# A decoder layer in one kernel: the eight scatters of a token tile go in three groups behind TensorE's signals, and VectorE normalises the probabilities ahead of the first query bias

## The chip, the cores and the metric

The kernel runs on one core of a Trainium2 chip. The metric is the device time of one execution in microseconds (us). Before the change three timed runs gave 1859.75 to 1864.37 us, median 1863.71.

## What is computed

The reference is a decoder layer on 4096 tokens (64 sequences of 64) of 256 numbers, with a layer norm after each of three parts:

```python
x = layernorm(x + self_attention(x))          # causal, one head, its own norm ahead of it and its own residual
x = layernorm(x + cross_attention(x, ctx))    # 16 query heads, 4 key/value heads, RMS norm of q and k
x = layernorm(x + ffn(x))                     # 64 experts, the 8 best of each token, and a shared expert

# cross attention
q = rmsnorm(x @ Wq + bq); k = rmsnorm(ctx @ Wk + bk); v = ctx @ Wv + bv
out = softmax(q @ k.T * scale + mask) @ v @ Wo
# ffn
logits = x @ gate_w.T; topv, topi = top_k(logits, 8); w = softmax(topv)
out = sum_e w_e * (silu(x @ g_e.T) * (x @ u_e.T)) @ d_e.T + sigmoid(x @ s) * shared(x)
```

## The kernel before

The work is in three phases: attention with routing, experts, and the sum of the experts' results. The change is in the first.

**Tiles and steps.** The 4096 tokens are 32 tiles of 128. A step of the attention phase works on six tiles at once, each in another stage: a is the newest tile, then b, c, d, e, f, each one tile older. `pipeline` writes out the first six and the last steps and runs those between as a loop with two steps in its body; half way (behind `MIDDLE`) the loop is cut, and VectorE has three more operations in `place` for each tile from there on. For each engine a function `step` lists by hand what it does in a step, in order; engines wait for each other on semaphores alone. Each engine works its list strictly in order, so whatever stands behind a wait waits too.

**TensorE in a step.** The part around the change: it transposes the self attention's result of c (`x1_transpose`) and the normalised input rows of a (`x_transpose`, L594, signal `xn_transposed`), multiplies the joined heads of e with Wo (`cross_output`, L754, 48 matmuls, signal `cross_proj`), and projects the queries of c in four groups of four heads (`query_project`, L602, signal `q_projected`). The fourth group reuses the PSUM bank of the first, and so waits until VectorE has added the first bias (`q_biased`). Then come the transposes of the self attention's probabilities of b and the cross attention's of d (`cross_probs_transpose`, L729, behind `cross_probs`), the key and value projections of c, the first product with the values of d, and, in the next step, the transposes of the normalised queries (`query_transpose`, L699) in two halves: the first behind VectorE's `query_norm` (L1037), the second behind POOL's `scale_queries` (L537).

**VectorE in a step.** Behind the choice of the experts' slots (`place`, whose last operation L1185 sorts the eight slots of a token into the row buffer, signal `slots_sorted`), it masks the cross scores of d and subtracts the maximum, sums the exponentials (`cross_sum`), adds the residual of e to the product with Wo and takes its moments (`x2_add`, L1080 and following), adds the first two query biases (L1027), normalises the probabilities of d (`cross_normalise`, L1067), takes the low part of the context (`ctx_low`, L944), adds the other two biases, and goes on with sums of squares, the key's bias and the norm of the first half of the queries.

**ScalarE** squares the queries group by group behind each bias and takes the high part of the context (`ctx_high`), on which `ctx_low` waits.

**POOL (GpSimd) in a step.** It computes the reciprocal roots as powers (L507: for keys, input, residuals, and the queries in two halves), scales keys and the second half of the queries, and scatters tile f: each token's row of 272 numbers goes to the eight slots of its experts in DRAM, by eight indirect DMAs of 128 rows each (`scatter`, L562), whose descriptors POOL writes. Ahead of the first stand four waits for the parts of the row. `wait_alone` is a wait that also counts up a semaphore that nobody reads, so that it stays an instruction of its own. Six scatters stand ahead of `power_h2` (the root for e's residual norm) and two behind it; then come the powers of the queries of c.

**SyncE** loads inputs and stores rows, and in the first half of the loop also clears pages of the slot table in DRAM.

## Time and profile before

| | us |
|---|---|
| median of three timed runs | 1863.71 |
| their range | 1859.75 to 1864.37 |
| profiled execution: span from first to last instruction | 1858.0 |
| attention phase, up to about | 1120 |
| expert phase, up to about | 1746 |
| sum of the experts' results, to the end | 1858 |

The page gives no own time of the profiled execution beside its span; the span stands 5.7 us under the median of the timed runs. In the profile, an engine's row carries its start, its length, the engine, the line, the operation with what it writes and reads, and in brackets how long the engine had been idle before it and what ended that. TensorE's ends are modelled: its row tells when its work should be done, not when its signal reached another engine. A row of POOL's scatter tells how long POOL wrote descriptors, not how long the rows travelled.

### The profile page before, as it was taken

How to read it: one execution, taken by the hardware profiler on the slowest of the kernel's cores; microseconds unless marked ns; L12 is line 12 of the kernel's file. 1: busy time of each engine (PE TensorE's matmuls, PEld its weight loads, DVE VectorE, ACT ScalarE, POOL GpSimd, SP SyncE). 2: the span in 40 equal slices, each digit the busy share in tenths (PEclk: the TensorE clock that was granted, in tenths of full speed). 3: DMA queues.
4: the chain of work that ended last, by engine and by line, in shares of the span. 5: the costliest groups of instructions: out<-in, count | busy, mean ns of one | idle time of the engine just before them, and what ended most of it. 6: DMA issues, size and time to landing. Idle time of an engine off the chain costs nothing. (4 is left out here: it accounts for less than half of the span.)

```text
span 1858.0 us, 34769 instructions
## 1 busy us (share of the span) xinstructions
PE 1532.2 (82%) x9744; PEld 1252.6 (67%) x9744; DVE 1259.3 (68%) x3827; ACT 688.5 (37%) x1526; POOL 1050.2 (57%) x1023
## 2 busy tenths in 40 slices
PE   4899989899998898989999864787877777777696
PEld 3688878777787787878788753565655555555464
DVE  3788888787888888888888744345555555433397
ACT  3444444343444434344343412232322322322254
POOL 3457666676766666666676633555555455555321
PEclk8799999999999999999999866889898998988799
DMA  7422232222222121211212484655555555554596
GB/s 248 136 81 100 80 102 68 91 86 89 90 85 96 46 74 51 67 60 46 82 45 73 101 280 139 192 162 154 163 178 165 177 165 162 175 170 137 189 418 281
DMA packets 182739, 246.40 MB, mean 133 GB/s; under 512 B 30732, under 2 KB 159321, under 8 KB 178148
## 3 DMA queue, kind: packets, MB, share of 16 engines
q1 hardware_dynamic: 148948, 169.71, 29.4%
q0 software_dynamic: 27648, 69.28, 10.2%
q10 hardware_dynamic: 6032, 6.13, 1.0%
q8 instruction: 46, 0.75, 0.2%
q14 instruction: 65, 0.53, 0.1%
HBM read 136.19 MB, written 117.19 MB: 136 GB/s over the span
## 5 line engine op out<-in xcount | busy, mean ns | idle before, releaser
L1571 POOL DMA_INDIRECT expert_out_scratch<-y,target x320 | 316.6, 989 | 297.7 <-DVE y L1797 199.9
L562 POOL DMA_INDIRECT slot_scratch<-xrow x256 | 260.5, 1018 | 188.9 <-DVE xrow L1185 117.4
L1630 PE MATMUL bank_g<-gu,x_turned 128*128 (+1 forms) x1408 | 218.8, 305 | 15.9 <-issue 13.7
L1630 PEld LDWEIGHTS bank_g<-gu,x_turned 128*128 128x128 f32 x1408 | 196.8, 216 | 30.8 <-issue 30.4
L1689 ACT ACTIVATE x_turned<-bank_x 128x512 f32<-128x512 f32 x176 | 105.3, 599 | 281.1 <-PE bank_x L1612 161.3
L1649 PE MATMUL bank_y<-dp,inter_t 64*128 (+1 forms) x352 | 136.8, 473 | 84.7 <-DVE y L1797 59.5
L507 POOL TENSOR_TENSOR q_rs<-q_ve,minus_half 128x8 f32<-128x8 f32 x64 | 137.4, 2147 | 114.9 <-DVE q_ve L1016 111.4
L754 PE MATMUL bank_d<-wo_w,o2t 128*128 128x256 f32 x1536 | 196.0, 288 | 2.0 <-DVE o2t L944 2.0
L754 PEld LDWEIGHTS bank_d<-wo_w,o2t 128*128 128x128 f32 x1536 | 190.3, 196 | 2.7 <-DVE o2t L944 2.7
L1788 DVE TENSOR_TENSOR inter<-silu,bank_g 128x128 f32<-128x128 f32 x176 | 50.2, 285 | 207.6 <-ACT silu L1696 144.9
L1797 DVE COPY y<-bank_y 128x512 f32<-128x512 f32 x160 | 110.2, 689 | 103.9 <-remote 72.0
L602 PE MATMUL bank_c<-wq_w,x1t 128*128 128x512 f32 x576 | 147.8, 401 | 24.5 <-DVE q_work L1027 21.2
L828 ACT ACTIVATE q_work<-q_work 128x512 f32<-128x512 f32 x128 | 80.0, 631 | 219.3 <-DVE q_work L1027 182.5
L1612 PE MATMUL bank_x<-identity,x_rows 128*128 128x128 f32 x704 | 127.7, 309 | 24.6 <-DMA x_rows<-token_row_scratch 24.6
L1612 PEld LDWEIGHTS bank_x<-identity,x_rows 128*128 128x128 f32 x704 | 82.7, 153 | 90.6 <-issue 90.6
L602 PEld LDWEIGHTS bank_c<-wq_w,x1t 128*128 128x128 f32 x576 | 105.9, 191 | 54.7 <-DVE q_work L1027 30.0
L1649 PEld LDWEIGHTS bank_y<-dp,inter_t 64*128 64x128 f32 x352 | 57.3, 203 | 121.9 <-issue 121.3
L1651 PE MATMUL bank_y<-dp,inter_t 64*128 64x256 f32 x352 | 137.5, 474 | 0.0
L719 PEld LDWEIGHTS bank_c<-k2t,stage_b 128*128 128x128 f32 x1024 | 123.2, 200 | 11.3 <-issue 11.3
L719 PE MATMUL bank_c<-k2t,stage_b 128*128 128x64 f32 x1024 | 127.7, 286 | 0.4 <-ACT stage_b L817 0.4
L699 PE MATMUL bank_c<-identity,q_work 128*128 128x128 f32 x512 | 70.5, 282 | 47.8 <-DVE q_work L1037 45.1
L1696 ACT ACTIVATE silu<-bank_g 128x128 f32<-128x128 f32 x176 | 49.1, 279 | 153.1 <-PE bank_g L1630 106.7
(245 smaller groups left out, 3412.6 us busy)
## 6 DMA issues: line engine op xcount, KB each, us to landing
x_rows<-slot_scratch SPq DMA_DIRECT2D x320, 136.0 KB
results<-expert_out_scratch SPq DMA_DIRECT2D x32, 1024.0 KB, 8.8
slot_scratch<-zeros SPq DMA_DIRECT2D x16, 816.0 KB, 4.2
dp<-in_down SPq DMA_DIRECT2D x161, 64.0 KB
slot_scratch<-zeros SPq DMA_DIRECT2D x8, 1088.0 KB, 9.1
gu<-in_gate_up SPq DMA_DIRECT2D x11, 768.0 KB
expert_out_scratch<-y,target POOLq DMA_INDIRECT x320
token_row_scratch<-xrow SPq DMA_DIRECT2D x32, 136.0 KB
```

The costliest lines, as they stand in the source:

```text
L507: nc.gpsimd.tensor_tensor(out_, base, minus_half[:, 0:width], ALU.pow).then_inc(sig[done], 1)
L562: nc.gpsimd.indirect_dma_start(out=slot_d[:, :], out_offset=bass.IndirectOffsetOnAxis(ap=xrow[slot][:, SLOT8 + k:SLOT8 + k + 1].bitcast(U3 ...
L602: last = nc.tensor.matmul(target, left[a][:, c, :], right(b, c), start=(n == 0 and c == 0), stop=(n == len(PASSES) - 1 and c == C - 1))
L719: last = nc.tensor.matmul(bank_c[:, n, p * S:(p + 1) * S], q2t[:, n, 2 * p:2 * p + 2, :].rearrange("p h s -> p (h s)"), k2t[:, p // 2, n * ...
L754: last = nc.tensor.matmul(bank_d[:, 0, 0:D], o2t[a][:, h, :], wo_w[b][:, h, :], start=(n == 0 and h == 0), stop=(n == len(PASSES) - 1 and ...
L1571: nc.gpsimd.indirect_dma_start(out=y_d[:, :], out_offset=bass.IndirectOffsetOnAxis(ap=target[n % 8][:, j:j + 1], axis=0), in_=y[s % 4][:, ...
L1612: mm = nc.tensor.transpose(bank_x[:, s % 2, (2 * j + c) * P:(2 * j + c + 1) * P], x_in[s % 8][:, j, c * P:(c + 1) * P], identity[:, :])
L1630: mm = nc.tensor.matmul(bank_g[:, s % 2, j * P:(j + 1) * P], xt[s % 2][:, j, c, :], w, start=(c == 0), stop=(c == C - 1))
L1649: nc.tensor.matmul(bank_y[:, 0, 0:D], inter_t[s % 2][0:INNER, :], dp[0:INNER, bass.ds(own, D)], start=True, stop=True)
L1651: nc.tensor.matmul(bank_y[:, 1, 0:D], inter_t[s % 2][INNER:P, :], dp[INNER:P, ring * D:(ring + 1) * D], start=True, stop=True).then_inc(si ...
L1689: nc.scalar.activation(xt[s % 2][:, :, :, :].rearrange("p j c n -> p (j c n)"), bank_x[:, s % 2, :], ACT.Copy).then_inc(sig["x_copied"], 1)
L1797: nc.vector.tensor_copy(y[s % 4][:, :, :], bank_y[:, :, 0:D])\
```

## The change

It has three parts. On POOL the eight scatters are split into four, two and two. The four now also wait until TensorE has transposed the input rows of tile a, the next two until it has finished the output projection of e, and the last two, which stood directly behind `power_h2`, until it has finished the fourth query projection of c. On VectorE the normalisation of the probabilities and the context's low part go ahead of the first two query biases. On ScalarE the context's high part goes ahead of the first square.

```diff
@@ POOL, step
                 at(d, bias_values)
-                for k in range(6):
+                at(a, turned_rows)
+                for k in range(4):
+                    at_slot(f, scatter, k)
+                at(e, joined_heads)
+                for k in range(4, 6):
                     at_slot(f, scatter, k)
                 at(e, power_h2)
+                at(c, joined_queries)
                 for k in range(6, TOP_K):
                     at_slot(f, scatter, k)
                 at(c, power_queries, 0)
...
+            def turned_rows(t):
+                wait_alone(pool, sig["xn_transposed"], t + 1, sig["pool_held"])
+
+            def joined_heads(t):
+                wait_alone(pool, sig["cross_proj"], t + 1, sig["pool_held"])
+
+            def joined_queries(t):
+                wait_alone(pool, sig["q_projected"], 4 * t + 4, sig["pool_held"])
@@ ScalarE, step
-                at(c, square_queries, 0)
                 at(c, ctx_high)
+                at(c, square_queries, 0)
                 at(c, square_queries, 1)
@@ VectorE, step
                 at(e, x2_add)
+                at(d, cross_normalise)
+                at(c, ctx_low)
                 at(c, query_bias, 0)
                 at(c, query_bias, 1)
-                at(d, cross_normalise)
-                at(c, ctx_low)
                 at(c, query_bias, 2)
```

POOL in the loop, from the value bias of d to the first power of the queries of c. `slot_scratch` is the slot table in DRAM, `xrow` the row buffer, `h_rs` and `q_rs` the roots. Before:

```order
L551 TENSOR_TENSOR v<-v_new,bkv_b 128x512 [waits cross_out,v2_copied]
L101 REGISTER_ALU
L562 DMA slot_scratch<-xrow 208897x272 [waits x2_normed,token_named,shared_gate,slots_sorted]
L562 DMA slot_scratch<-xrow 208897x272 x5
L507 TENSOR_TENSOR h_rs<-h_ve,minus_half 128x1 [waits h2_var]
L562 DMA slot_scratch<-xrow 208897x272 x2
L506 ISA
L507 TENSOR_TENSOR q_rs<-q_ve,minus_half 128x8 [waits q_var]
```

And in the changed kernel:

```order
L551 TENSOR_TENSOR v<-v_new,bkv_b 128x512 [waits cross_out,v2_copied]
L562 DMA slot_scratch<-xrow 208897x272 [waits xn_transposed,x2_normed,token_named,shared_gate,slots_sorted]
L562 DMA slot_scratch<-xrow 208897x272 x3
L562 DMA slot_scratch<-xrow 208897x272 [waits cross_proj]
L562 DMA slot_scratch<-xrow 208897x272
L507 TENSOR_TENSOR h_rs<-h_ve,minus_half 128x1 [waits h2_var]
L101 ISA
L562 DMA slot_scratch<-xrow 208897x272 [waits q_projected]
L562 DMA slot_scratch<-xrow 208897x272
```

Two scatters more stand behind a signal of the output projection, and the last two behind one of the query projections; the powers stand where they stood.

VectorE in the loop, from the sum of the exponentials of d to the first sum of squares of c. `stage_b` holds the probabilities, `q_work` the queries, `ctxt` the context. Before:

```order
L1063 RECIPROCAL s_rec<-s_sum 128x16 [waits cross_sum]
L1080 TENSOR_TENSOR h<-x_res,bank_d 128x256 [waits x1_res_loaded,cross_proj]
L947 BN_STATS h_stat<-h 128x6 [waits h2_done]
L949 BN_AGGR h_mv<-h_stat 128x2 [waits h2_stats]
L951 TENSOR_SCALAR h_ve<-h_mv 128x1 [waits h2_moments]
L1027 TENSOR_TENSOR q_work<-bank_c,bq_b 128x512 [waits q_projected] x2
L1067 TENSOR_TENSOR stage_b<-stage_b,s_rec 128x1024 [waits cross_recip]
L944 TENSOR_TENSOR ctxt<-ctx_in,ctxt 128x256 [waits ctx_hi]
L1027 TENSOR_TENSOR q_work<-bank_e,bq_b 128x512 [waits q_projected]
```

And in the changed kernel, whose lines there are numbered 14 higher:

```order
L965 TENSOR_SCALAR h_ve<-h_mv 128x1 [waits h2_moments]
L1081 TENSOR_TENSOR stage_b<-stage_b,s_rec 128x1024 [waits cross_recip]
L958 TENSOR_TENSOR ctxt<-ctx_in,ctxt 128x256 [waits ctx_hi]
L1041 TENSOR_TENSOR q_work<-bank_c,bq_b 128x512 [waits q_projected] x2
L1041 TENSOR_TENSOR q_work<-bank_e,bq_b 128x512 [waits q_projected]
```

The normalisation and the context's low part now stand between the moments of the residual and the first query bias, and nothing stands between the second bias and the third.

## Rows read from the trace of the kernel before

**Rows 1.** Busy time of each engine in the window 161 to 1007 us.

```profile
core 0: us, PE busy (x) PEld busy (x) DVE busy (x) ACT busy (x) POOL busy (x), PEclk, DMA share, GB/s
161.00:1007.00 846.00, 768.50 (x5230) 669.56 (x5229) 697.05 (x1662) 358.10 (x702) 564.28 (x517) 0.99 0.22 75
```

**Rows 2.** Timeline of TensorE: starts of the cross output projection in four steps.

```profile
161.55 0.71 PE L754 MATMUL bank_d<-wo_w,o2t 128*128 128x256 f32 x4
944.26 0.95 PE L754 MATMUL bank_d<-wo_w,o2t 128*128 128x256 f32 x6
975.07 1.20 PE L754 MATMUL bank_d<-wo_w,o2t 128*128 128x256 f32 x8
1038.50 1.19 PE L754 MATMUL bank_d<-wo_w,o2t 128*128 128x256 f32 x8
```

**Rows 3.** Waits, 161 to 1007 us: total, times, longest.

```profile
PE bank_c L699 <- DVE q_work L1037: 36.3, 24, 2.0
DVE h L1080 <- remote: 31.6, 14, 3.3
PE bank_c L602 <- DVE q_work L1027: 21.2, 20, 1.6
PE bank_d L729 <- DVE stage_b L1067: 17.4, 10, 2.3
```

**Rows 4.** Timeline of TensorE, 500 to 600 us: start, length, idle before.

```profile
517.13 0.38 PE L594 MATMUL bank_a<-identity,x_n 128*128 128x128 f32 x2
517.27 6.00 PE L754 MATMUL bank_d<-wo_w,o2t 128*128 128x256 f32 x48
528.77 1.68 PE L602 MATMUL bank_c<-wq_w,x1t 128*128 128x512 f32 x6 [1.40 <-DVE q_work L1027]
549.58 5.99 PE L754 MATMUL bank_d<-wo_w,o2t 128*128 128x256 f32 x48
564.78 1.09 PE L729 MATMUL bank_d<-identity,stage_b 128*128 128x128 f32 x8 [2.26 <-DVE stage_b L1067]
```

**Rows 5.** Timeline of VectorE, 500 to 570 us.

```profile
516.86 0.23 DVE L1185 MAX8 xrow<-meta 128x8 uint32<-128x64 f32 x1
526.67 0.42 DVE L1080 TENSOR_TENSOR h<-x_res,bank_d 128x256 f32<-128x256 f32 x1 [3.24 <-remote]
528.03 1.29 DVE L1027 TENSOR_TENSOR q_work<-bank_c,bq_b 128x512 f32<-128x512 f32 x2
529.23 1.22 DVE L1067 TENSOR_TENSOR stage_b<-stage_b,s_rec 128x1024 f32<-128x1024 f32 x1
530.70 0.68 DVE L1027 TENSOR_TENSOR q_work<-bank_e,bq_b 128x512 f32<-128x512 f32 x1
536.18 1.21 DVE L1037 TENSOR_TENSOR q_work<-q_work,q_rs 128x1024 f32<-128x1024 f32 x1
557.22 0.42 DVE L1080 TENSOR_TENSOR h<-x_res,bank_d 128x256 f32<-128x256 f32 x1 [0.36 <-remote]
```

**Rows 6.** Timeline of POOL, 500 to 600 us, and one scatter at 955.

```profile
517.98 1.06 POOL L562 DMA_INDIRECT slot_scratch<-xrow  x1 [2.44 <-DVE xrow L1185]
521.94 0.97 POOL L562 DMA_INDIRECT slot_scratch<-xrow  x1 [0.31 <-issue]
524.49 0.98 POOL L562 DMA_INDIRECT slot_scratch<-xrow  x1 [0.30 <-issue]
528.92 1.04 POOL L562 DMA_INDIRECT slot_scratch<-xrow  x1 [0.20 <-issue]
533.40 1.81 POOL L507 TENSOR_TENSOR q_rs<-q_ve,minus_half 128x8 f32<-128x8 f32 x1 [2.11 <-DVE q_ve L1016]
536.35 2.55 POOL L507 TENSOR_TENSOR q_rs<-q_ve,minus_half 128x8 f32<-128x8 f32 x1
555.36 0.98 POOL L562 DMA_INDIRECT slot_scratch<-xrow  x1 [0.30 <-issue]
955.14 1.72 POOL L562 DMA_INDIRECT slot_scratch<-xrow  x1 [0.19 <-issue]
```

More of the change, by code:

```diff
@@ L912, in step @@
                 at(d, cross_exp)
+                at(c, ctx_high)
                 at(c, square_queries, 0)
-                at(c, ctx_high)
                 at(c, square_queries, 1)
```

## The prediction

> **What bounds the kernel now.** I read the windows first, then the waits of the attention loop, and the timelines of TensorE, VectorE and GpSimd (POOL) over two neighbouring steps. In the window 161 to 1007 us, which holds 26 steady steps of the attention loop, TensorE is busy 768.5 of 846.0 us, 91%, and every other engine less [rows 1]. The change touches nothing outside that loop, so I need the step: from 161.55 to 1038.50 us TensorE starts the cross output projection 28 times, which makes 27 steps of 32.48 us [rows 2].
>
> The waits say where TensorE stands still in those steps: 36.3 us before the transposes of the queries (L699, for VectorE's normalised queries), 21.2 us before the fourth query projection (L602, for a query bias), 17.4 us before the transposes of the probabilities (L729, for their normalisation) [rows 3]. 74.9 us in all is the most that this change can reach. The fourth row shows why: 14 times VectorE sat before its residual add, 31.6 us in all, for a "remote" event.
>
> The timeline of one step names that event. TensorE's output projection starts at 517.27 and takes 6.00 us, so it ends at 523.27 (I call this moment T0) [rows 4]. VectorE's add, which waits for it, starts at 526.67, 3.4 us later, after 3.24 us idle [rows 5]. In the next step the projection ends at 555.57 and the add starts at 557.22, 1.65 us later. So the lateness is none of TensorE's own work; it comes and goes. What moves against T0 is POOL's train of scatters: it starts at 517.98, the fourth at 521.94, the sixth at 524.49 [rows 6], and the add starts 2.2 us behind the sixth; in the next step T0 falls into the fourth scatter, of 555.36, and the add starts 1.9 us behind that one. I read it so: **a long train of scatters holds back TensorE's completion signals until the train has drained.** The bias behind the add is late, and with it the fourth projection, which starts at 528.77 = T0 + 5.5 [rows 4].
>
> **The change, part by part.**
>
> *Normalisation ahead of the first query bias (VectorE).* In the second step the normalisation stands behind two late biases, and TensorE waits 2.26 us for it [rows 4]. Behind the add it is done some 3 us after the add, before the fourth projection ends. The 17.4 us go. In return the first bias starts later by what normalisation and the context's low part take, 529.23 to 530.70 = 1.47 us [rows 5], and the fourth projection waits for that bias. ScalarE's swap only makes the context's high part early enough for this; ScalarE idles there, so it costs nothing.
>
> *Four scatters behind the turned rows (POOL).* The transposes of x end at 517.13 + 0.38 = 517.51 [rows 4]. From the last signal to the first scatter POOL needs 0.89 us (slots sorted at 516.86 + 0.23, scatter at 517.98) [rows 5, 6]. The new wait stands ahead of four satisfied ones, so the first scatter starts at 518.4 to 518.6 instead of 517.98, the fourth 3.96 us behind it, at 522.4 to 522.6. T0 still falls into the fourth. The train now ends there. Its signal then comes 1.9 to 2.2 us after the fourth start (the two values above): 1.0 to 1.5 us after T0. Where VectorE sorts the slots later than that (in the second half of the loop it has three more operations ahead of them), the wait costs nothing and the whole train is later. I take the add at T0 + 1.5.
>
> *Two scatters behind the output projection.* They start 0.9 us after its signal, when the first train has drained; such a pair on its own held nothing in the traced step (scatters from 528.92 on, and VectorE's rows show no idle time from 528.03 to 536.18). The power for the residual's norm waits behind them, until about T0 + 4.8; its reader on VectorE stands behind the fourth bias, which can't start before T0 + 6.8, so it costs nothing. If the second bias's signal were caught by them, rival 3 has the price.
>
> *Two scatters behind the last query projection.* That projection ends at 528.77 + 1.68 = 530.45 (call it G) [rows 4]. The pair starts at G + 0.9 and takes one period and one length, (524.49 - 521.94) / 2 + 1.04 = 2.3 us [rows 6]; the first power of the queries can start at G + 3.2. Now it starts at 533.40 = G + 2.95. The chain behind it on POOL (two powers, the key's square and scale, the second half's scale) sets TensorE's second transposes, so +0.25 us a step is the upper bound. Against it stands this: the biases 3 and 4 no longer wait behind the normalisation, so VectorE starts its norm of the queries (536.18, G + 5.7) as soon as the first power ends, about G + 5.0 [rows 5]. POOL's second power took 2.55 us where it started 0.17 us behind that norm, the first 1.81 us [rows 6]. In the new order it starts at G + 6.1, when the norm is nearly over; if overlap is what lengthens it, it gains 0.7 us and the step 0.45. Between +0.25 and -0.45 I take 0, as nothing in this trace shows the second power without the norm.
>
> The Trainium skill (SBUF — State Buffer, "SBUF: two separate sides") says that a VectorE operation with two inputs in SBUF and a GpSimd operation that reads SBUF exclude each other for the whole instruction. The 2.55 us agree with it; by the rule alone the step would be 0.45 us shorter still, 27 times that is 12 us, and the forecast 1835.5.
>
> **The sum.** New step: add at T0 + 1.5; add to bias, 526.67 to 528.03 = 1.36 [rows 5]; normalisation and context 1.47; bias to fourth projection, 528.03 to 528.77 = 0.74; together 5.1. That projection 1.68. From its end to the next T0 (530.45 to 555.57) 25.1. In all 31.88 us against 32.48, 0.60 us less; over 27 steps 16.2 us. The span goes from 1858.0 to 1841.8. The median of the timed runs, 1863.7, lies 5.7 above the span; taken along, **1847.5 us** (0.9% less). The own range of this case, with the add between T0 + 1.2 and T0 + 1.9 and the chain within -0.45 and +0.25, is 1827 to 1865, most of it below 1858. A measurement of this kernel tells about 0.3%, 5.6 us, from no change.
>
> **Rivals.**
>
> *1. The signals come at once.* Four scatters may be too few to hold TensorE. For it: a step exists in which TensorE never waits for a bias nor for probabilities, from 944.26 to 975.07, 30.81 us [rows 2]. Against it: in the second step the signal was caught in the fourth scatter already. All steps at 30.8 give 27 x 1.67 = 45 us less: about 1818.
>
> *2. Slower: the lateness does not come from the scatters.* Then the add stays where it is, on the average of the two steps T0 + 2.5, and the 1.47 us put ahead of the first bias hit the fourth projection in full: 2.5 + 1.36 + 1.47 + 0.74 = 6.1, a step of 6.1 + 1.68 + 25.1 = 32.9, 0.4 more than now, 27 times that is 11 us: 1874.5. It decides from an add at about T0 + 2.1 on. Against it: the lateness ends 2 us after a scatter's start in both steps.
> The Trainium skill (same page and section) says that the engines' ports and the DMAs' are separate and that a DMA cannot be slowed by a compute operation, nor the reverse. By that rule scatters would not touch TensorE's signals and this rival would hold; the 3.24 us of [rows 5] speak against reading it so widely.
>
> *3. Nothing gained: POOL becomes the limit.* The last pair starts 0.9 us behind G, and if it catches the key projection's signal, which falls into it, or stretches under VectorE's work, as the first scatter of such a pair did at 955.14 (1.72 us for 1.04) [rows 6], the power moves to G + 3.6 or later. With +0.6 on the chain the gain is gone: 32.48, that is about 1864. For it: POOL's chain from the first power to the second half's scale has no slack, since TensorE's 36.3 us of [rows 3] hang on it.
>
> **Numbers.** My forecast 0.50, rival 1 0.17, rival 2 0.13, rival 3 0.20. The forecast's case is nearly all faster by more than 5.6 us, rival 1 wholly, rival 3 mostly same, rival 2 slower: faster 0.64, same 0.20, slower 0.16. The range takes in rival 1 down to 1814 and rival 2 up to its centre, 1874.
>
> **What would show it.** In the profile of the changed kernel: the wait L729 for the normalisation gone; VectorE's idle time before the residual add 1 to 1.5 us a step instead of 0.4 to 3.3; TensorE's wait before the fourth query projection 0.9 to 1.1 us in nearly every step (near nothing: rival 1; 1.5 and more: rival 2); the first query power at G + 3.2 and the second shorter than 2.55 us or not; the step 31.9 us. TensorE waiting for POOL's scale of the queries before the second transposes would be rival 3. I am wrong if the signals of the second and third projection are held by the middle pair, or if the step shrinks by more than 1 us.

## The result, and the profile after

| | before | changed |
|---|---|---|
| median of the timed runs, us | 1861.82 (20 runs) | 1867.22 (20 runs) |
| their range | 1848.98 to 1872.33 | 1858.24 to 1873.57 |
| span of the profiled execution | 1858.0 | 1871.6 |

The changed kernel is slower by 0.4%: ratio 1.0038, 95% interval 1.002 to 1.0057. Forecast were 1847.5 us and 0.9% less. Of the 13.6 us between the two spans, 5.6 lie in the 27 steps of the loop, 2.1 before them and 5.8 behind the last one, where the change touches nothing; those last two vary from run to run, as the medians differ by 5.4 us alone, no more than the loop. So the question is why the 16.2 us did not come.

In the changed kernel line numbers in the loop are 14 higher: L768 is the output projection, L616 the query projection, L713 the transposes of the queries, L743 those of the probabilities.

Timeline of TensorE of the changed kernel, first and last start of the output projection, against [rows 2]:

```profile
163.69 0.48 PE L768 MATMUL bank_d<-wo_w,o2t 128*128 128x256 f32 x2
1046.26 0.96 PE L768 MATMUL bank_d<-wo_w,o2t 128*128 128x256 f32 x6
```

882.57 / 27 = 32.69 us a step, against 32.48 before and 31.88 forecast. The 27 steps as a window, before and then changed (columns as in [rows 1]):

```profile
161.55:1038.50 876.95, 794.82 (x5406) 692.02 (x5405) 723.80 (x1722) 370.35 (x725) 584.66 (x534) 0.99 0.22 74
```

```profile
163.70:1046.20 882.50, 805.86 (x5405) 707.09 (x5403) 743.96 (x1724) 371.93 (x725) 593.32 (x534) 0.97 0.22 74
```

The granted clock is the news: 0.97 where it was 0.99. For the same 5406 matmuls TensorE is busy 805.9 us instead of 794.8, 11.1 more. The waits, 161 to 1007 us (total, times, longest), against [rows 3]:

```profile
PE bank_c L713 <- DVE q_work L1051: 50.0, 26, 2.1
PE bank_c L616 <- DVE q_work L1041: 19.4, 18, 1.6
DVE h L1094 <- PE bank_d L768: 7.5, 12, 0.8
DVE h L1094 <- remote: 3.0, 8, 0.4
```

The wait for the probabilities (17.4 us) is gone, VectorE's wait before the add fell from 31.6 to 10.5 us, and the wait for a bias stayed near 20. The wait before the transposes of the queries grew by 13.7 us. Waits alone make the kernel faster by 17.4 + 1.8 - 13.7 = 5.5 us. The 11.1 us of longer busy time outweigh that, and the difference, 5.6 us, is what the loop grew by.

Timeline of TensorE over two neighbouring steps (start, length, idle before):

```profile
519.31 5.99 PE L768 MATMUL bank_d<-wo_w,o2t 128*128 128x256 f32 x48
529.48 1.66 PE L616 MATMUL bank_c<-wq_w,x1t 128*128 128x512 f32 x6
538.56 1.07 PE L713 MATMUL bank_c<-identity,q_work 128*128 128x128 f32 x8 [1.99 <-DVE q_work L1051]
539.60 2.34 PE L616 MATMUL bank_a<-qkv_w,xnt 128*128 128x512 f32 x12
550.48 6.00 PE L768 MATMUL bank_d<-wo_w,o2t 128*128 128x256 f32 x48
561.64 1.68 PE L616 MATMUL bank_c<-wq_w,x1t 128*128 128x512 f32 x6 [1.06 <-DVE q_work L1041]
570.66 1.77 PE L713 MATMUL bank_c<-identity,q_work 128*128 128x128 f32 x8 [1.89 <-DVE q_work L1051]
572.51 3.17 PE L616 MATMUL bank_a<-qkv_w,xnt 128*128 128x512 f32 x12
584.21 5.99 PE L768 MATMUL bank_d<-wo_w,o2t 128*128 128x256 f32 x48
```

The first step is 31.17 us long, the second 33.73. In the second the fourth projection waits 1.06 us for its bias, as forecast, and 1.89 us of idle time follow before the transposes; then these take 1.77 us for 1.07, and the projection behind them 3.17 for 2.34. The windows of the two places say why (the 0.55 is the clock):

```profile
539.60:544.00 4.40, 4.40 (x32) 3.99 (x31) 2.73 (x12) 3.14 (x8) 4.32 (x5) 1.00 0.00 0
570.50:574.00 3.50, 3.34 (x14) 3.08 (x15) 2.57 (x7) 1.05 (x2) 3.42 (x4) 0.55 0.00 0
```

TensorE ran at 1.2 GHz there. 13 of the 27 steps have such a stretch, against 4 before. As (1 - granted clock) x length, summed over it, the loop lost 23.9 us to it, before 6.8. That is an upper measure: what runs slowly ahead of a wait only shortens the wait. In the kernel before two steps with the same wait for the probabilities (2.1 us) took 27.18 us from G, the end of the fourth query projection, to the next T0 with such a stretch behind it, and 27.14 without: the wait for the queries, 1.4 us in the second, was gone in the first; in the changed kernel the stretches stand behind the last long wait, and a step takes 26.87 instead of 25.3.

Timeline of POOL, the same two steps, against [rows 6] (four, two, two):

```profile
520.83 1.06 POOL L562 DMA_INDIRECT slot_scratch<-xrow  x1 [3.49 <-issue]
525.01 0.98 POOL L562 DMA_INDIRECT slot_scratch<-xrow  x1 [0.30 <-issue]
526.69 0.97 POOL L562 DMA_INDIRECT slot_scratch<-xrow  x1 [0.70 <-issue]
532.14 1.04 POOL L562 DMA_INDIRECT slot_scratch<-xrow  x1 [2.21 <-PE bank_c L616]
534.47 1.69 POOL L507 TENSOR_TENSOR q_rs<-q_ve,minus_half 128x8 f32<-128x8 f32 x1
...
556.24 0.97 POOL L562 DMA_INDIRECT slot_scratch<-xrow  x1 [0.30 <-issue]
566.53 1.71 POOL L507 TENSOR_TENSOR q_rs<-q_ve,minus_half 128x8 f32<-128x8 f32 x1
568.20 1.05 POOL L533 TENSOR_TENSOR k2s<-k 128x512 f32<-128x512 f32 x1
569.37 2.55 POOL L507 TENSOR_TENSOR q_rs<-q_ve,minus_half 128x8 f32<-128x8 f32 x1
```

And VectorE:

```profile
525.94 0.42 DVE L1094 TENSOR_TENSOR h<-x_res,bank_d 128x256 f32<-128x256 f32 x1 [0.72 <-PE bank_d L768]
536.19 2.07 DVE L1051 TENSOR_TENSOR q_work<-q_work,q_rs 128x1024 f32<-128x1024 f32 x1 [0.62 <-POOL q_rs L507]
558.12 0.42 DVE L1094 TENSOR_TENSOR h<-x_res,bank_d 128x256 f32<-128x256 f32 x1 [0.39 <-remote]
567.72 1.57 DVE L1030 TENSOR_SCALAR q_ve<-q_ss 128x8 f32<-128x8 f32 x1
569.20 1.21 DVE L1051 TENSOR_TENSOR q_work<-q_work,q_rs 128x1024 f32<-128x1024 f32 x1
```

The add stands at T0 + 0.6 and T0 + 1.6 (T0 = 525.30, 556.48). In the second step (G = 563.32) the first power starts at G + 3.2 and ends at 568.24, but the norm of the queries starts 0.96 us later, at G + 5.9: VectorE still stands in L1030, 1.57 us long where the same operation for the first half takes 0.17, until POOL's square of the keys (568.20 + 1.05) is done. In the first step (G = 531.14) the norm starts as the power ends, at G + 5.05, and takes 2.07 us for 1.21. Either way it ends at G + 7.1. Each of the 27 steps is of one kind or the other: 20 have the long L1030 (1.6 to 1.8 us), 7 the long norm.

### The profile page after: what moved, and what is told of

Its sections match the earlier page's. It is cut to its first block and busy times, and to the rows that moved or that the text cites. A ratio compares the mean times of both kernels' runs of the same rounds, so it can differ in the third digit from the quotient of the medians.

```text
span 1871.6 us, 34891 instructions
## 1 busy us (share of the span) xinstructions
PE 1547.4 (83%) x9744; PEld 1269.1 (68%) x9744; DVE 1279.8 (68%) x3827; ACT 690.5 (37%) x1526; POOL 1060.4 (57%) x1023
## 5 line engine op out<-in xcount | busy, mean ns | idle before, releaser
L562 POOL DMA_INDIRECT slot_scratch<-xrow x256 | 270.1, 1055 | 280.4 <-issue 101.5
L768 PE MATMUL bank_d<-wo_w,o2t 128*128 128x256 f32 x1536 | 196.5, 289 | 2.0 <-DVE o2t L958 2.0
L768 PEld LDWEIGHTS bank_d<-wo_w,o2t 128*128 128x128 f32 x1536 | 190.7, 196 | 2.7 <-DVE o2t L958 2.7
L616 PE MATMUL bank_c<-wq_w,x1t 128*128 128x512 f32 x576 | 150.9, 408 | 24.1 <-DVE q_work L1041 20.3
L616 PEld LDWEIGHTS bank_c<-wq_w,x1t 128*128 128x128 f32 x576 | 107.2, 194 | 56.2 <-DVE q_work L1041 29.0
L713 PE MATMUL bank_c<-identity,q_work 128*128 128x128 f32 x512 | 75.5, 296 | 62.5 <-DVE q_work L1051 60.1
L713 PEld LDWEIGHTS bank_c<-identity,q_work 128*128 128x128 f32 x512 | 61.9, 151 | 69.0 <-issue 54.3
```

What stands on the lines that cost most here:

```text
L562: nc.gpsimd.indirect_dma_start(out=slot_d[:, :], out_offset=bass.IndirectOffsetOnAxis(ap=xrow[slot][:, SLOT8 + k:SLOT8 + k + 1].bitcast(U3 ...
L616: last = nc.tensor.matmul(target, left[a][:, c, :], right(b, c), start=(n == 0 and c == 0), stop=(n == len(PASSES) - 1 and c == C - 1))
L713: last = nc.tensor.transpose(bank_c[:, h // 4, (h % 4) * P:(h % 4 + 1) * P], q2s[:, n * half + h, :], identity[:, :])
L768: last = nc.tensor.matmul(bank_d[:, 0, 0:D], o2t[a][:, h, :], wo_w[b][:, h, :], start=(n == 0 and h == 0), stop=(n == len(PASSES) - 1 and ...
```

## The experiments

T0 and G are as in the prediction. "Half clock" is the time lost to it in all 27 steps, by the upper measure above. The kernels ran on three chips; each is compared with the kernel before on its own chip. On which chip the first profiles were taken is not on record; by its time, 1862 us, it is like chip 1. The changed kernel was not run on chip 1, and the kernel before was timed there but has no trace.

| kernel | chip | ratio to before (95%) | step | fourth projection at T0 + | first power at G + | G to next T0 | half clock |
|---|---|---|---|---|---|---|---|
| before (first profile) | | | 32.48 | 4.90 | 3.7 | 25.95 | 6.8 |
| changed (first profile) | | 1.0038 | 32.69 | 4.87 | 3.3 | 26.16 | 23.9 |
| e1, groups only | 1 | 0.978 (0.975 to 0.981) | 31.48 | 4.25 | 3.3 | 25.66 | 6.8 |
| e2, normalisation only | 1 | 1.010 (1.006 to 1.014) | 33.47 | 6.44 | 2.3 | 24.79 | 34.1 |
| e3, changed, wait filled | 1 | 0.989 (0.985 to 0.993) | 32.09 | 4.97 | 3.3 | 25.49 | 3.4 |
| e4, before, wait filled | 1 | 1.001 (0.998 to 1.004) | 32.71 | 5.22 | 3.4 | 25.81 | 8.5 |
| e5, changed, keys squared on ScalarE | 2 | 1.007 (1.004 to 1.009) | 30.64 | 4.46 | 3.3 | 24.55 | 3.4 |
| e6, before, the same | 2 | 0.988 (0.985 to 0.991) | 29.71 | 3.97 | 2.4 | 24.21 | 1.7 |
| e7, changed again | 3 | 1.033 (1.031 to 1.036) | 32.30 | 4.52 | 3.3 | 26.15 | 23.9 |
| e8, groups only, the same square | 3 | 0.998 (0.996 to 1.000) | 30.09 | 3.95 | 3.3 | 24.60 | 1.7 |
| e9, one wait | 3 | 1.001 (0.998 to 1.003) | 30.17 | 3.97 | 2.4 | 24.66 | 1.7 |
| e10, two waits | 3 | 1.016 (1.013 to 1.019) | 31.02 | 3.97 | 3.3 | 25.52 | 5.1 |
| e11, before again | 3 | one run | 30.17 | 3.97 | 2.4 | 24.67 | 1.7 |
| e12, e6 again | 3 | 0.988 (0.986 to 0.990) | 29.73 | 3.97 | 2.4 | 24.22 | 1.7 |
| e13, e8 again | 3 | 0.996 (0.994 to 0.998) | 30.09 | 3.95 | 3.3 | 24.60 | 1.7 |
| e14, one wait, the same square | 3 | 0.989 (0.987 to 0.990) | 29.73 | 3.97 | 2.4 | 24.22 | 1.7 |
| e15, normalisation only, again | 3 | 1.008 (1.005 to 1.011) | 30.66 | 4.66 | 2.2 | 24.37 | 0 |
| e16, e14 again | 3 | 0.994 (0.992 to 0.996) | 29.73 | 3.97 | 2.4 | 24.22 | 1.7 |

Columns four to seven are means over the 27 steps of one profile. The kernel before took a median of 1880.11 us on chip 1, 1619.21 on chip 2 and 1617.62 to 1622.72 on chip 3.

**e1, the groups alone.** The change without its edits on VectorE and ScalarE:

```diff
-                at(d, cross_normalise)
-                at(c, ctx_low)
                 at(c, query_bias, 0)
                 at(c, query_bias, 1)
+                at(d, cross_normalise)
+                at(c, ctx_low)
```

> POOL's groups as in the change, VectorE's and ScalarE's order as before. Theory A (the lost time is TensorE's clock: in the changed kernel the wait before the query transposes is 1.9 us instead of 1.6, and in 13 of 27 steps the granted clock then falls to 1.2 GHz for one stretch of 3.4 us, 1.6 us a step): the wait before the transposes stays at or above 1.9 us where the query power starts at G + 3.2, the dips come as in the changed kernel or fewer where other waits share the step; the probabilities' wait L729 comes back with 10 to 17 us; span 1860 to 1880. Theory B (the groups alone are worth their time, the order of VectorE costs it): faster than before by 5 to 15 us.

1835.45 us, 45 less than the kernel before on this chip: more than theory B's 5 to 15, and nothing of theory A's 1860 to 1880. TensorE's waits from the first to the last start of the output projection:

```profile
PE bank_c L713 <- DVE q_work L1051: 47.8, 27, 2.5
PE bank_c L616 <- DVE q_work L1041: 6.6, 5, 1.8
PE bank_d L743 <- DVE stage_b L1081: 1.7, 2, 0.9
```

The waits for a bias and for probabilities are nearly gone without the new order on VectorE. Grouping alone is worth 2.2% on this chip, and the wait before the transposes is nearly as long as in the changed kernel (1.8 us a step against 1.9), so it is not the new order that makes it; e9 and e10 show the last pair of scatters in its place.

**e2, the normalisation alone.** The kernel before with only the edits on VectorE and ScalarE.

> VectorE's and ScalarE's order as in the change, POOL's six and two as before. Both theories: the output projection's signal is late by up to 3.3 us again, so the fourth query projection starts at T0 + 6.1 in such steps and waits 2 us. Theory A: 0.4 us a step more than before, about 11 us slower than before, and dips follow the longer waits. Theory B: slower than the changed kernel by as much as the groups are worth.

1896.49 us. TensorE's waits, same stretch:

```profile
PE bank_c L602 <- DVE q_work L1027: 62.4, 26, 3.4
PE bank_c L699 <- DVE q_work L1037: 18.9, 27, 1.9
```

With signals late, each bias is 1.5 us later still: the wait for it triples against [rows 3]. The wait behind it shrinks, but more than the 17.4 us for the probabilities is given back, and 20 of 27 steps have a half-clock stretch, most of them over the late fourth projection, which takes up to 2.9 us there for 1.7.

**e3 and e4, the wait filled.** 13 transposes of the identity matrix, into a bank that the queries' transposes overwrite, stand in the wait before these; e3 on the changed kernel, e4 on the one before. The extra transposes are work the reference does not ask for.

```diff
+                    for k in range(FILL):
+                        nc.tensor.transpose(bank_c[:, 0, 0:P], identity[:, :], identity[:, :])
+                pe.wait_ge(sig["q_normed_b" if n else "q_normed_a"], t + 1)
```

> The changed kernel with 13 transposes of the identity, whose result nobody reads, in TensorE's wait before the query transposes (about 1.4 of the 1.9 us). Every other wait and order is as in the change. Theory A: the dips of the granted clock in the loop go from 13 steps to 3 or fewer, the steps with a dip (33.7 us) become 31.2 to 32.2 us, and the time falls by about 10 x 1.6 = 16 us or more below the changed kernel, so below before as well. Theory B (the clock falls for another reason and has no part in it): the time stays within 4 us of the changed kernel.

> The kernel before with the same 13 transposes in the same wait. Theory A: before has only 4 steps with a dip in the loop, so at most 4 x 1.6 = 6 us are to be had; where the wait is 1.5 us, 13 transposes of 0.11 us just fill it. Gain 2 to 7 us. If filling is worth the same here as in the changed kernel, the clock isn't what separates the two.

e3 took 1858.03 us, e4 1879.16. The waits and the windows of the loop, e3 and then e4:

```profile
PE bank_c L617 <- DVE q_work L1043: 23.5, 19, 1.8
PE bank_c L715 <- DVE q_work L1053: 8.9, 27, 0.5
```

```profile
167.31:1033.62 866.31, 827.73 (x5757) 727.25 (x5756) 751.85 (x1722) 370.82 (x725) 591.42 (x534) 1.00 0.22 75
```

```profile
166.46:1049.65 883.19, 836.55 (x5758) 729.54 (x5756) 723.76 (x1722) 369.24 (x725) 582.79 (x534) 0.99 0.22 74
```

Nothing that VectorE or POOL do in e3 is earlier (add at T0 + 1.34, first power at G + 3.3, norm over at G + 7.1, as in the changed kernel), TensorE only does more; yet the step falls from 32.69 to 32.09, since one step instead of 13 has a half-clock stretch. That is 0.60 x 27 = 16 us, about what theory A gave. The two steps compared come from different runs and perhaps chips, but the steps of the changed kernel's own trace agree (26.87 against 25.3 from G to the next T0, as above). The same filling gives the kernel before nothing that stands clear of the noise (1.001, of 2 to 7 us expected); the clock costs it little. So the clock is the greater part of what went missing. Even so e3 stays 1.2% behind e1 on the same chip: that is the price of the new order on VectorE.

**e5 and e6, the keys squared on ScalarE.** POOL's square of the keys goes to ScalarE, e5 on the changed kernel, e6 on the one before:

```diff
             def square_keys(t):
-                pool.wait_ge(sig["k_biased"], t + 1)
-                nc.gpsimd.tensor_tensor(k2s[:, :, :], k2[:, :, :], k2[:, :, :], ALU.mult).then_inc(sig["k_squared"], 1)
+                act.wait_ge(sig["k_biased"], t + 1)
+                nc.scalar.activation(k2s[:, :, :], k2[:, :, :], ACT.Square).then_inc(sig["k_squared"], 1)
```

> The changed kernel with the squares of the keys taken by ScalarE (behind its copy of the values) instead of by POOL between the two query powers. Theory A': the norm of the queries on VectorE (two inputs in SBUF) starts 0.96 us behind the first power because POOL's key square, which reads SBUF, stands there first and shuts it out; without it the norm starts at G + 5.0 instead of G + 5.9 and TensorE's wait before the query transposes falls from 1.9 to about 1.0 us; POOL's chain is shorter by up to 1.03 us too. The step falls by 0.8 to 1.0 us and the dips of the clock become rare: 30 to 45 us less than the changed kernel. Rival: the norm waits for something else (it stays at 0.96 behind the power); then only POOL's chain gets shorter and, as that has 0.2 us of slack, the step stays within 0.3 us.

> The same edit on the kernel before. Theory A': norm of the queries at G + 4.9 instead of G + 5.7 at best, as VectorE's own chain (biases 3 and 4 behind the normalisation, which the change had moved) takes until then: 0 to 0.8 us a step, 0 to 20 us less than before. If the change's order is worth what it was meant to be, the fifth kernel is faster than this one by 10 us or more.

These two fell on another chip, on which the kernel before needs 1619.21 us. VectorE and POOL in e5, one step:

```profile
510.64 0.69 DVE L1041 TENSOR_TENSOR q_work<-bank_c,bq_b 128x512 f32<-128x512 f32 x1 [0.67 <-PE bank_c L611]
515.62 1.23 DVE L1051 TENSOR_TENSOR q_work<-q_work,q_rs 128x1024 f32<-128x1024 f32 x1 [0.58 <-POOL q_rs L507]
```

```profile
513.88 3.32 POOL L507 TENSOR_TENSOR q_rs<-q_ve,minus_half 128x8 f32<-128x8 f32 x2
```

The norm starts at G + 5.0 in every step now and takes 1.23 us: what my forecast gave it with the square still on POOL. The wait before the transposes is 1.0 us instead of 1.9, and one step has a half-clock stretch instead of 13. e6 beats the kernel before by 1.2%; e5 stays behind it, and behind e6 by 1.9%, the reverse of the 10 us that the change was to be worth. How much e5 gains on the changed kernel itself can't be said, as that was not run on this chip.

The two powers of e5 also answer what the forecast left open. The second one starts 0.06 us ahead of the norm and takes 1.64 us, with the norm at 1.23 beside it. In e6, where it starts 0.17 us behind the norm in all steps but one, it takes 2.55. So not the overlap lengthens it: it depends on which of the two starts first.

**e7 to e10, the parts on a third chip.** e7 is the changed kernel. e8 is e1 with the square on ScalarE. e9 and e10 are e1 with fewer waits:

```diff
-                at(a, turned_rows)
```

in e10, and in e9 also

```diff
-                at(c, joined_queries)
```

> The changed kernel itself, as the measure for the three others on the same chip. 0.2 to 0.6% slower than before, with 10 or more steps of the loop that have a stretch at 1.2 GHz.

> The four, two, two of POOL with VectorE's and ScalarE's order as before (the first experiment's kernel), and the keys squared by ScalarE. Theory: the fourth query projection starts at T0 + 3.95 without a wait in the first half of the loop, and the norm of the queries directly behind the first power: TensorE's wait before the query transposes 1.0 us instead of 1.8, a step 29.9 us instead of 30.8, 20 to 28 us under the first experiment's kernel, if both are run on one chip. Rival: without POOL's key square the second power starts beside the norm and takes 2.55 us again, and the chain's slack is used up; then 10 us or less.

> As the first experiment, but only the wait for the output projection's signal is kept, between the fourth scatter and the fifth; the first four and the last two wait for no signal of TensorE. Theory C (a pause before the fifth scatter is what frees the signal): the add starts at T0 + 0.1 to 1.8 as in the first experiment, and the fourth projection at T0 + 3.95. The last two scatters follow the residual's power at once: query power back at G + 2.95, the step 0.1 to 0.3 us shorter, unless the four scatters in a row hold the signals of the third and fourth projection (biases 3 and 4 late by 1 to 2 us, 0.5 to 1.5 us a step more). So 0.972 to 0.980 of before, or up to 1.00 if they do.

> As the first experiment without the wait for the transposed input rows. Theory C: that wait moves the first scatter by 0 to 0.8 us (from 0.47 to 1.28 us behind the transposes in every second step) and no signal of TensorE falls between; without it the four are over earlier, so the add in those steps is as prompt as with it or more so: within 0.3% of the first experiment's 0.978. If the wait matters, the add is late by 1 us or more in every second step and the ratio is above 0.985.

1673.77, 1617.21, 1621.03 and 1644.26 us, the kernel before 1618.48. Here the change costs 3.3%, where 0.2 to 0.6% was expected. Of 0.972 to 0.980 for e9 and about 0.978 for e10 nothing came either: both counted on the gain of chip 1. The wait for the output projection ahead of the fifth scatter costs nothing and gains nothing (e9). The wait for the queries ahead of the last pair, with which e10 is at 1.016 and without which e9 is at 1.001, costs 1.4%: the first power moves from G + 2.4 to G + 3.3, and with it the next T0 by 0.86 us.

**e11, the kernel before on that chip.**

> The kernel before, for its trace on this chip. If this chip is one of those on which the kernel before needs about 1619 us, both theories expect that TensorE's signals come within 0.1 us of its modelled ends all through the train of six scatters, that the fourth query projection starts at T0 + 3.95 in nearly every step, and that the first query power starts at G + 2.2 to 2.4 (T0: end of the output projection, G: end of the fourth query projection). If it is one that needs 1860 to 1880 us: signals late by up to 3 us behind the fourth scatter, fourth projection at up to T0 + 5.5, as in the first trace. A third outcome, late signals together with a short time or the reverse, would part the two and say that the chip's slowness is not what makes the signals late.

1616.6 us, in one run. An output projection and VectorE around its end, and POOL's train in the same step:

```profile
490.63 6.00 PE L754 MATMUL bank_d<-wo_w,o2t 128*128 128x256 f32 x48
496.52 0.25 DVE L1063 RECIPROCAL s_rec<-s_sum 128x16 f32<-128x16 f32 x1
496.77 0.42 DVE L1080 TENSOR_TENSOR h<-x_res,bank_d 128x256 f32<-128x256 f32 x1
```

```profile
491.34 1.06 POOL L562 DMA_INDIRECT slot_scratch<-xrow  x1 [2.45 <-DVE xrow L1185]
496.57 0.97 POOL L562 DMA_INDIRECT slot_scratch<-xrow  x1 [0.30 <-issue]
497.85 0.97 POOL L562 DMA_INDIRECT slot_scratch<-xrow  x1 [0.31 <-issue]
```

T0 is 496.63, and the six scatters stand against it as they do in the first step of [rows 4, 6]: the fifth just ahead of it, the sixth 1.22 us behind. There the add came 3.40 us after T0, here it comes 0.14 us after it, with POOL at the fifth scatter and the sixth still to come. TensorE's waits from first to last start:

```profile
PE bank_c L699 <- DVE q_work L1037: 29.1, 27, 1.5
PE bank_e L711 <- DVE logits L1099: 3.7, 1, 3.7
```

No wait for a bias, none for probabilities: the 21.2 and 17.4 us of [rows 3], which the change was to work on, do not exist on this chip. The signals are late on one chip and punctual on another, with the same program; a train of scatters alone does not make them late. Nor are the scatters slower to travel on the one than on the other: from 161 to 977 us their 9600 packets took 9.3% of the 16 DMA engines' time before, and in e11 10368 took 10.0%, the same for each.

**e12 to e14, what could beat both.** The square on ScalarE in the kernel before (e12, as e6), with the groups (e13, as e8), and with one wait (e14, e9 with the square).

> The kernel before with the keys squared on ScalarE. Theory C, that VectorE's norm of the queries stands behind POOL's square of the keys on any chip: about 1 us a step less, 27 steps, on 1619 us a ratio of 0.985 to 0.990 as before. On a chip with late signals the power itself starts later, the norm behind it, and the same 1 us a step remains: 0.983 to 0.990. Rival D, that the gain is a smaller share of TensorE at half clock: nothing on a chip where the kernel before keeps its clock.

> Grouped scatters alone, with the keys squared on ScalarE. On a chip whose signals are not late, theory (grouping gains nothing there and the last pair's wait puts the first power at G + 3.2 instead of G + 2.2): within 0.4% of the kernel before, the two edits cancelling. On a chip whose signals are late: both gain, 0.960 to 0.970. Rival (the two edits take the same idle time): no better than the grouping alone, 0.978.

> Scatters behind one signal only (the fifth behind the output projection, the other seven as before), normalisation where it was before, keys squared on ScalarE. On a chip without late signals: that of the key square alone, 0.985 to 0.990, as one wait there cost nothing. On a chip with late signals: the first train is four, so the first biases come as with the full grouping, and the first power is not held to G + 3.2: 0.955 to 0.970, the best of all. Rival: the train of four that follows the wait catches the signal of the third projection, and the result is no better than the kernel before with the key square.

1601.75, 1616.39 and 1603.62 us, the kernel before 1622.72. Moving the square is worth 1.2% on two chips; in the kernel before it saves 0.45 us a step rather than the full 1 us, 12 of the 21 us between the medians, so that the ratio fell into the expected range in part by luck. The 0.45 are just what the norm of the queries gains in the mean of the steps (G + 5.11 to G + 4.66); there VectorE's own list sets when it starts. In e12 it directly follows L1016:

```profile
534.05 0.17 DVE L1016 TENSOR_SCALAR q_ve<-q_ss 128x8 f32<-128x8 f32 x1
534.13 1.22 DVE L1037 TENSOR_TENSOR q_work<-q_work,q_rs 128x1024 f32<-128x1024 f32 x1
```

The full grouping gives 0.8 of that back. None of the three was run on chip 1, so whether one wait with the square is the best where signals are late stays open.

**e15 and e16.** e2 and e14 again.

> Only the normalisation ahead of the first query bias, scatters six and two as before. On a chip without late signals: normalisation and context put 0.6 to 1.3 us ahead of the fourth query projection (T0 + 4.5 to 5.2 instead of 3.95), the first power stays at G + 2.2, so no half-clock stretches are added: 27 steps by 0.6 to 1.3 us are 16 to 35 us, a ratio of 1.010 to 1.022. That and the 1.6% which the last pair's wait cost there make up the 3.3% of the changed kernel. Rival: the clock falls here as well (10 steps or more with a half-clock stretch) and the ratio is 1.025 or more, which would make the order on VectorE alone the cause of the fall. On a chip with late signals: 1.010 as in the first run.

> One wait (fifth scatter behind the output projection), normalisation where it was, keys squared on ScalarE. On a chip without late signals 0.985 to 0.990, as before. On a chip with late signals 0.955 to 0.970: the first train is four scatters there, the biases come at T0 + 1.5 and 3.1 as with the full grouping, and the norm of the queries follows the first power at once. Rival: the six scatters behind the fourth run into one another there and hold the signals of the third and fourth query projection, 0.985 or more.

1627.76 and 1609.07 us, the kernel before 1617.62. The new order on VectorE costs 0.8% here, with no half-clock stretch at all, less than the 1.010 that I gave as the lower end: in about half of the steps of the loop's first half the bias has room. e16 is 0.6% faster than before, outside the 0.985 to 0.990 expected, and e14, the same program, 1.1%, with intervals that just miss each other. Their steps are alike to the hundredth (29.73); e16's median is 5 us higher and that of the kernel before 5 us lower than in e14's comparison. So half a per cent between two such comparisons tells nothing of the loop.

## Why the prediction was wrong

**On the chip of the first profile.** By its own sum, 5.1 + 1.68 + 25.1 = 31.88:

- *The fourth projection at T0 + 5.1.* Measured 4.87 in the mean of 27 steps, 4.1 to 4.2 and 5.2 by turns in the first half. With its length G stands at T0 + 6.53, against 6.78. Right, a little on the safe side: the add came at T0 + 1.34 instead of 1.5, where its mean before was 2.31. The train of four does let the signal through earlier. But the mean of the fourth projection had been 4.90 before: by its own terms the forecast gained nothing here, and all of its 0.6 us came from the last term, 25.1 where the mean had been 25.95. Of that 0.85 the wait for the probabilities is 18.4 / 27 = 0.68 (its total over the 27 steps).
- *The wait for the probabilities goes.* Right, and so is the bias's wait of 0.9 to 1.1 us in the steps that have one. But in e1 the groups alone ended nearly all of both waits, with G at T0 + 5.83. The new order on VectorE, which I took for the means, was not needed for it and put G 0.7 us later (0.64 on chip 3, by e7 against e10).
- *From G to the next T0 25.1.* **This is the step that failed**: it took 26.16. The forecast had TensorE at full clock throughout and POOL's chain at no cost. Three things make the 1.06. The clock: of steps alike in their waits, those with a half-clock stretch take 26.87, the others 25.3; ten take 26.87 and two 26.1 and 26.5, and (10 x 1.57 + 2.0) / 27 = 0.66. The one step half way through the loop, 30.8 (before 29.9), adds 5.5 / 27 = 0.2: I took an ordinary step for the mean, while the 32.48 that I set it against held the odd one. The rest, 0.2, is the last pair ahead of the first power, the upper bound of +0.25 that I had set against a gain of 0.45.
- *The norm of the queries at G + 5.0.* It was over at G + 7.1 instead of 6.2. I saw that the biases no longer hold VectorE there, and missed POOL's key square, which starts as the power ends and costs the norm 0.9 us, as a late start or as a long run. It had its part before, too: the 0.97 us from the end of the first power to the norm in [rows 5, 6], which I read as the biases' doing, shrink to 0.4 or 0.7 in e6 without the square. e5 moved the square away, and both were gone: all norms took 1.23 us, all L1030 0.17. The second power, which I wanted shorter, stayed at 2.55 us. The Trainium skill (SBUF — State Buffer, "SBUF: two separate sides") has the rule that I had cited for the other pair: VectorE's norm has two inputs in SBUF and POOL's square reads SBUF, so one excludes the other; the 2.07 us for 1.21 agree with it. For the power it holds one way only: the norm, which started 0.06 us behind it in e5, took no longer for that. I had applied it to the operation that I wanted gone and not to its neighbour.

With G 0.25 earlier than forecast the sum is 31.88 - 0.25 + 0.66 + 0.2 + 0.2 = 32.69, as measured.

What makes the clock fall can be told only by what stood before, and only in part. Leave out the step half way through the loop:

| TensorE's waits in a step | runs | steps | with a fall |
|---|---|---|---|
| 0.3 to 1.7 us before the fourth projection, then 1.7 to 2.0 before the transposes | changed, e7 | 35 | 22 |
| 1.7 to 2.2 us before the transposes alone | changed, e1, e7, e10 | 63 | 4 |
| 0.8 to 1.6 us, then 1.4 to 1.6 | before | 14 | 0 |
| 0.3 to 1.2 us, then 0.8 to 1.0 | e15 | 21 | 0 |

(e1 has four more with both, two of them with a fall.) So a second wait goes with the fall, but the sum of the two does not decide: up to 3.2 us in the third row never did it, and in the first row steps alike to 0.1 us fell or didn't. In the kernel before three of its four falls stood behind a wait of 2.1 to 2.3 us for the probabilities. The forecast removed idle time in one place and did not ask what stood next to the idle time it left. e3 shows that it is the idle time of TensorE: filled, it costs no clock.

**The mechanism.** That a long train of scatters holds TensorE's signals was half of it. On chip 1 it fits the gain of 2.2% by grouping, though without a trace of the kernel before on that chip the 45 us can't be split into steps. But the same trains hold nothing on chip 3 (e11), so the scatters are an occasion and something in the chip the condition. I can't say what; the expert phase, which has trains of scatters too, is where those chips differ most (from the last start of [rows 2] to the end of the span 819 us, in e11 638), and there VectorE's copy out of PSUM waits for a "remote" event on the one and for its own transfers on the other. From the same view, waits from 1100 to 1600 us, before and then e11:

```profile
DVE y L1797 <- remote: 53.0, 29, 3.0
```

```profile
DVE y L1797 <- DMA expert_out_scratch<-y,target: 26.3, 23, 4.1
```

**On chip 3** the cost adds up from run to run: the last pair behind the queries 0.86 us a step (e10 against e9, which equals e11); the new order puts G at T0 + 6.15 instead of 5.51, 0.64 (e7 against e10); and from G to the next T0 e7 needs 26.15 us, e10 25.52, 0.63 more, which the 11 falls of the clock that e10 doesn't have account for, at 1.58 us each (17.4 / 27 = 0.64). Together 2.13, as measured (32.30 - 30.17), or 57 us, and the medians differ by 55.3. Order and last pair alone cost 0.8% (e15) and 1.6% (e10); the rest of the 3.3% comes only when both stand together.

**The rivals.** Rival 1, a step of 30.8 us, is what e1 shows in 19 of its 27 steps (30.4 to 31.0): the groups without the new order reach it there. Rival 2 (slower) had the right sign for a wrong reason: the add was not later. Rival 3, POOL as the limit, came nearest: the last pair did move the first power, to G + 3.3. The range of my own case, 1827 to 1865, missed the result by 2 us; that 1814 to 1874, with the rivals, held it is no merit, as none of them had the clock in it. For the same reason the chance of "slower", 0.16, was too small.

## What to carry to other kernels

Ask of each wait that is left what else stands in the same step: a wait of 1.9 us with another ahead of it cost TensorE its clock in 22 of 35 steps, one alone in 4 of 63, and the stretch at half speed cost more (1.6 us) than the wait that went with it (1.06). A stretch at half speed ahead of a wait costs next to nothing, so ask where it falls before it is priced. Set a forecast of one step against the mean of the steps, term by term: here that would have shown at once that the whole gain hung on one term. Before two edits are made together, price each alone: here one was worth 2.2% on one chip, the other cost 1.0%, and on chip 3 both together brought falls of the clock in 13 steps, where either alone had none or two. And a gain that rests on a timing which the program does not set, such as a late signal, has to be measured on more than one chip; the work taken off an engine that excludes another (the key square) held its gain on both chips it was tried on.

## What the runs showed of the hardware

- The same program takes 1862 to 1880 us on some chips and 1618 to 1622 on others; the loop's step is 32.48 or 30.17 us, the rest after it 819 or 638.
- On the slower ones VectorE waits up to 3.3 us for signals of TensorE behind a train of scatters [rows 3]; on the faster one traced with this program it doesn't (e11).
- A wait of 1.7 to 2.2 us alone in a step went with a fall of TensorE's clock to 1.2 GHz in 4 of 63 steps (changed, e1, e7, e10), one of 1.7 to 2.0 us with a shorter one ahead of it in 22 of 35 (changed, e7), and pairs of up to 1.6 and 1.6 us in none of 14 (before). A fall behind the last long wait of a step cost 1.6 us, one ahead of it next to nothing (27.18 against 27.14, before).
- A square of 128x512 numbers on POOL (1.05 us) lengthened VectorE's norm from 1.21 to 2.07 us (7 steps of the changed kernel), or a VectorE operation on 128x8 numbers, L1030, from 0.17 to 1.6 to 1.8 (the other 20 steps); with the square on ScalarE neither happened (e5). The latter has one input only, so two inputs are not needed for it. By its row it starts 0.5 us ahead of the square and ends with it, which stays unexplained.
- POOL's power of 128x8 numbers took 2.55 us when it started 0.17 us behind VectorE's norm, and 1.64 when it started 0.06 us ahead of it, with the norm at 1.23 (e5, e6).
